# State-space attention and expert layer on one core: B and C of batch 0 by TensorE, halves of delta and du, an earlier last W1 piece, one exponential in PSUM

## The reference, cut to what matters

```python
z = layernorm(x)                                     # gate
u = silu(causal_conv4(in_proj @ ctx) + conv_b)       # 256 channels x 256 steps
dt_lo, Bm, Cm = split(x_proj @ u)                    # 8, 16 and 16 rows x 256 steps
delta = softplus(dt_proj @ dt_lo + dt_proj_b)
state = state * exp(delta[..., None] * A) + (delta * u)[..., None] * B_t     # over the steps, 16 states
y = (state . C_t + D * u) * silu(z);   x = x + y
f = layernorm(x);  probs = softmax(f @ router_w + router_b); top 6 of 32, renormed
x = x + mean of 2 shared experts(f) + sum_e gate_e * expert_e(f)             # relu(f W1 + b1) W2 + b2
```

## Time and profile before

| what | value |
|---|---|
| median of three runs | 386.52 us (384.69 to 386.78) |
| profiled execution | 384.17 us |
| its span | 382.40 us, granted TensorE clock 0.982 in the mean |
| busy: TensorE, VectorE, ScalarE, GpSimd | 358.6, 261.6, 216.7, 201.9 us |
| DMA | 54.20 MB, mean 142 GB/s |

### The profile page before, as it was taken

How to read it: one execution, slowest core, us unless ns; L and a number is a source line. 1 busy time by engine, 2 the same in 40 slices (tenths; PEclk the granted TensorE clock), 3 DMA queues, 4 the chain that set the end, 5 groups by cost and what they waited for, 6 DMA issues and landing times.

```text
span 382.4 us, 6892 instructions
## 1 busy us (share of the span) xinstructions
PE 358.6 (94%) x2301; PEld 320.4 (84%) x2301; DVE 261.6 (68%) x449; ACT 216.7 (57%) x539; POOL 201.9 (53%) x159
## 2 busy tenths in 40 slices
PE   6456889999999999999999999999999999999997
PEld 4233567898999898989999889989999899999996
DVE  3479988899988467499977556899763634344444
ACT  2867755768754445378644456496423346566662
POOL 0479998369993102389961011799830034444442
PEclk9959899999999999999999999999999999999999
DMA  7498871468523215897322235965232144233310
GB/s 233 133 329 240 214 239 44 117 220 283 162 76 87 68 53 136 252 287 206 97 79 82 63 122 155 338 196 141 82 84 82 43 141 139 82 86 89 106 57 27
DMA packets 30751, 54.20 MB, mean 142 GB/s; under 512 B 3298, under 2 KB 8580, under 8 KB 30724
## 3 DMA queue, kind: packets, MB, share of 16 engines
q1 hardware_dynamic: 30724, 53.86, 47.7%
HBM read 52.54 MB, written 1.31 MB: 141 GB/s over the span
## 4 chain that ended last, share of the span: by engine, by line
PE 84%; DMA 5%; DVE 5%; POOL 3%; ACT 2%; issue 1%; SPq 0%; DVEq 0%; POOLq 0%; ACTq 0%
PE acc L549 36%; PE z L570 12%; PE z L571 12%; PE z L572 12%; PE dA L549 4%; DMA bt<-bc 3%; PE acc L447 2%; DVE dA L777 1%; POOL w1l L916 1%; PE acc L556 1%; POOL bu L936 1%; PE misc L469 1%; DMA stage<-in_w 1%; PE dA L483 1%; PE dA L478 1%
## 5 line engine op out<-in xcount | busy, mean ns | idle before, releaser
L549 PE MATMUL acc<-hg,w 128*128 128x256 f32 x564 | 133.5, 379 | 0.0
L702 ACT ACTIVATE z<-z,par 128x256 f32<-128x256 f32 x188 | 75.7, 439 | 86.4 <-PE z L572 86.4
L570 PE MATMUL z<-xh,w1l 128*128 128x256 f32 (+1 forms) x376 | 118.5, 315 | 0.0
L936 POOL TENSOR_TENSOR bu<-bt,du 128x512 f32<-128x512 f32 x64 | 81.0, 1277 | 60.1 <-DMA bt<-bc 43.7
L549 PEld LDWEIGHTS acc<-hg,w 128*128 128x128 f32 x564 | 102.4, 190 | 11.2
L877 DVE TENSOR_TENSOR hg<-z,gt 128x512 f32<-128x512 f32 x88 | 60.5, 688 | 67.7 <-ACT z L702 66.9
L572 PE MATMUL z<-xh,w1h 128*128 128x256 f32 (+1 forms) x376 | 106.2, 282 | 0.0
L571 PE MATMUL z<-xl,w1h 128*128 128x256 f32 (+1 forms) x376 | 105.9, 282 | 0.0
L777 DVE TENSOR_TENSOR_SCAN dA<-dA,bu 128x512 f32<-128x512 f32 x64 | 78.2, 1222 | 9.7 <-POOL bu L936 8.9
L570 PEld LDWEIGHTS z<-xh,w1l 128*128 128x128 f32 x376 | 71.2, 189 | 5.9 <-issue 4.3
L571 PEld LDWEIGHTS z<-xl,w1h 128*128 128x128 f32 x376 | 70.7, 188 | 1.6
(11 more groups left out here) (130 smaller groups left out, 404.1 us busy)
## 6 DMA issues: line engine op xcount, KB each, us to landing
w<-in_w SPq DMA_DIRECT2D x92, 256.0 KB, 2.8
bt<-bc SPq DMA_DIRECT2D x32, 256.0 KB, 5.3
ct<-bc SPq DMA_DIRECT2D x32, 256.0 KB, 6.0
stage<-in_w SPq DMA_DIRECT2D x11, 512.0 KB, 6.8
gt<-gates SPq DMA_DIRECT2D x14, 128.0 KB
xr<-in_xr SPq DMA_DIRECT2D x4, 256.0 KB, 5.8
x<-in_xT SPq DMA_DIRECT2D x4, 256.0 KB, 5.0
out<-x SPq DMA_DIRECT2D x3, 256.0 KB, 7.0
```

Source lines behind the costliest of these rows:

```text
L549: mm = pe.matmul(total(b, k), weights, h, start=t + n == 0 and (k == 0 or final_batch(b)), stop=last, skip_group_check=True)
L570: pe.matmul(z[p % ZB][:, i, :], w1l[:, t, one], xh_, start=k == 0, stop=False)
L702: ins = act.activation(z[p % ZB][:, i, :], z[p % ZB][:, i, :], ACT.Relu, bias=b1[:, t:t + 1])
L936: pool.tensor_tensor(bu[:, r, :].rearrange("p (j l) -> p j l", j=2), bt[:, c % BRING], du[:, k:k + 1, :].broadcast_to([P, 2, L]), ALU.mult ...
```

## The change

- B and C of step 0 of batch 0 no longer come from HBM. A new TensorE step `rows`, behind `dt`, multiplies `xd` by columns of the identity, broadcast over 128 weight columns: each matmul writes one row of `xd` to all partitions, two rows of B to `z[1]`, two of C to `z[2]`. New ScalarE steps `bt0` and `ct0` copy them to `bt[:, 0]` and `ct[:, 0]`. The load `load_bc(0, 0)` goes; the spill stays.
- `delta` and `du` of batch 0 are made by halves. `bu(0,0)` waits for du of half 0 alone, `decay(0,0)` for both halves of delta, and the others for all as before.
- `rs1` moves from before the scans to step 0 (behind `ct0`), `nb1` to step 1, and one `w1h` from before the scans to step 0. Three `warm` steps of nine matmuls are added in steps 5 to 7.
- The last `w1h` and `w1l` move from behind `logits` to behind `econv` of batch 1, ahead of `uclip` and of the root `r2`.
- The exponential of `econv` of batch 1, and the `uclip` behind it, are written to `acc` in PSUM instead of `e1`; `spread`, which writes `acc` next, waits for `usig_done`.

```diff
-        ("dtl", 0), ("w1h", 0), ("w1l", 0), ("dt", 0), ("sp", 0), ("over", 0), ("rs1", 0), ("w1h", 0), ("delta", 0), ("nb1", 0)]
+        ("dtl", 0), ("w1h", 0), ("w1l", 0), ("dt", 0), ("rows", 0), ("sp", 0), ("over", 0), ("bt0", 0), ("delta", 0)]
...
-    HEAD += [(n, 0) for n in ((), (), ("zz",), ("ez1",), ("ez2",), ("ez3",), ("zmul",), ())[_c]]
-    HEAD += [("w1h", 0)] if _c in (1, 2, 4, 5) else []
+    HEAD += [(n, 0) for n in (("ct0", "rs1"), ("nb1",), ("zz",), ("ez1",), ("ez2",), ("ez3",), ("zmul",), ())[_c]]
+    HEAD += [("w1h", 0)] if _c in (0, 1, 2, 4, 5) else []
+    HEAD += [(("warm", None, 9), 0)] if _c > 4 else []
...
-         ("centre", 0), ("sq", 0), ("w1l", 0), (("taps", 3, KC), 1), ("var", 0), ("econv", 1), ("uclip", 1), ("r2", 0),
-         (("warm", None, 31), 0), ("norm", 0), ("usig", 1), ("xh", 0), ("logits", 0), ("w1h", 0), ("w1l", 0), ("u", 1), ("xl", 0),
+         ("centre", 0), ("sq", 0), ("w1l", 0), (("taps", 3, KC), 1), ("var", 0), ("econv", 1), ("w1h", 0), ("w1l", 0),
+         ("uclip", 1), ("r2", 0),
+         (("warm", None, 31), 0), ("norm", 0), ("usig", 1), ("xh", 0), ("logits", 0), ("u", 1), ("xl", 0),
...
-            load_bc(0, 0)
...
+                elif name == "rows":
+                    for row, bank in ((0, z[1]), (NS, z[2])):
+                        for j in range(2):
+                            mm = pe.matmul(bank[:, j, :], ident[0:NBC, row + j:row + j + 1].broadcast_to([NBC, P]), xd[0:NBC, :],
+                                           start=True, stop=True)
+                        mm.then_inc(S["rows_done"], 1)
...
+                    pe.wait_ge(S["usig_done"], 2)
...
-                    act.activation(e1[:], cv[:], ACT.Exp, scale=-1.0).then_inc(S["econv_done"], 1)
+                    act.activation(e_of(b)[:], cv[:], ACT.Exp, scale=-1.0).then_inc(S["econv_done"], 1)
...
-                        act.wait_ge(S["delta_done"], b + 1)
+                        if first(b) and k == 0:
+                            act.wait_ge(S["delta1_done"], 1)
+                        else:
+                            act.wait_ge(S["delta_done"], b + 1)
...
+                elif name == "bt0":
+                    act.wait_ge(S["rows_done"], 1)
+                    act.activation(bt[:, 0], z[1][:], ACT.Copy).then_inc(ld_b[0], 16)
+                elif name == "ct0":
+                    act.wait_ge(S["rows_done"], 2)
+                    act.activation(ct[:, 0], z[2][:], ACT.Copy).then_inc(ld_c[0], 16)
...
-                    dve.tensor_scalar(e1[:], e1[:], BIG, 1.0, ALU.min, ALU.add).then_inc(S["uclip_done"], 1)
+                    dve.tensor_scalar(e_of(b)[:], e_of(b)[:], BIG, 1.0, ALU.min, ALU.add).then_inc(S["uclip_done"], 1)
...
+                        fr.then(dve.tensor_tensor(delta[:, 0, :], xdt[:, 0, :], sp[:, 0, :], ALU.add))
+                        dve.tensor_tensor(du[:, 0, :], delta[:, 0, :], u[:, 0, :], ALU.mult).then_inc(S["du0_done"], 1)
+                        dve.tensor_tensor(delta[:, 1, :], xdt[:, 1, :], sp[:, 1, :], ALU.add).then_inc(S["delta1_done"], 1)
+                        dve.wait_ge(S["delta1_done"], 1)
+                        dve.tensor_tensor(du[:, 1, :], delta[:, 1, :], u[:, 1, :], ALU.mult).then_inc(S["delta_done"], 1)
...
-                        pool.wait_ge(S["delta_done"], b + 1)
+                        pool.wait_ge(S["du0_done" if first(b) and k == 0 else "delta_done"], 1 if first(b) and k == 0 else b + 1)
```

More of the change, by code:

```diff
@@ L216, in xattn_ffn_kernel @@
         aexp_done, aneg_done, const_done = sem("aexp_done"), sem("aneg_done"), sem("const_done")
-        names = ["xin_done", "conv_done", "econv_done", "u_done", "xall_done", "dtl_done", "bc_spilled", "dt_done", "abs_done", "wide_done", "half_done", "half_added", "spread_done",
+        names = ["xin_done", "conv_done", "econv_done", "u_done", "xall_done", "dtl_done", "bc_spilled", "dt_done", "abs_done", "rows_done", "delta1_done", "du0_done", "wide_done", "half_done", "half_added", "spread_done",
                  "v_done", "sp_done", "delta_done", "zz_done", "ez_done", "zmul_done", "bu_done", "da_ready",
@@ L308, in xin, with e_of @@
             return z[ZB - 1] if type(b) is int and b == 1 else misc
+        def e_of(b):
+            return acc if type(b) is int and b == 1 else e1
         def newton(b):
@@ L621, in step @@
                     act.wait_ge(S["uclip_done"], b + 1)
-                    fr.then(act.activation(e1[:], e1[:], ACT.Ln))
+                    fr.then(act.activation(e1[:], e_of(b)[:], ACT.Ln))
                     act.activation(e1[:], e1[:], ACT.Exp, scale=-1.0).then_inc(S["usig_done"], 1)
@@ L769, in step @@
                     fr.wait()
-                    fr.then(dve.tensor_tensor(delta[:], xdt[:], sp[:], ALU.add))
-                    dve.tensor_tensor(du[:], delta[:], u[:], ALU.mult).then_inc(S["delta_done"], 1)
+                    if first(b):
+                        fr.then(dve.tensor_tensor(delta[:, 0, :], xdt[:, 0, :], sp[:, 0, :], ALU.add))
[3 more added lines that the diff above has]
+                        dve.tensor_tensor(du[:, 1, :], delta[:, 1, :], u[:, 1, :], ALU.mult).then_inc(S["delta_done"], 1)
+                    else:
+                        fr.then(dve.tensor_tensor(delta[:], xdt[:], sp[:], ALU.add))
+                        dve.tensor_tensor(du[:], delta[:], u[:], ALU.mult).then_inc(S["delta_done"], 1)
                 elif name[0] == "scan":
```

## The result

Eight runs of the changed kernel took 383.29 to 384.88 us, with a median of 383.91; eight of the kernel before 384.08 to 387.10, with a median of 386.43. The ratio is 0.9947 (95% interval 0.9925 to 0.9968): 2.0 us faster by the ratio, 2.5 by the medians, where I had forecast 0.4. The median lies 0.5 us under the range.

The account below looks back on a forecast made before the run. TensorE was taken as busy throughout from 70 us, so only an earlier first-layer start counts. +0.1 us up to that start and -0.5 behind it give -0.4, 386.52 to 386.1 us; range 384.4 to 387.4.

Parts of the forecast that it names:

- part 3: Layer norm before the first layer: square gains 0.3 to 0.35 us, root waits for the last `w1h`, net +0.1 us.
- The front: First scans without the load of B: first product 0.7 us earlier, but scan(1,0) at 25.5, a loss of 0.25 us.
- The lock: VectorE instructions with two SBUF inputs wait for GpSimd's: `du1` ends at 20.35 instead of 19.5, `nb1` costs 0.8 us.
- GpSimd's end: All twelve w1l pieces done at 64.2 us; before, the eleventh ended at 63.84 and the twelfth at 67.55.
- The square: Square of the layer norm, held to 59.0 us before by a `w1h`; would start at 58.65, gaining 0.3 to 0.35.
- The root: `r2` on ScalarE, behind `econv` and the last `w1h`: starts at 60.85 us, against 60.76 before; the move's price is 0.45.
- The start of the first layer: First L570 matmul on TensorE, at 66.31 us before, forecast at 66.4.
- the cover: Before the Newton steps: `uclip`, 1.52 us before and 0.7 to 0.9 in PSUM, hidden until `r2` is ready at 61.71.
- The signs that I had set: Trace times to confirm the forecast, such as first scan 20.4, square 58.65, `nm` 0.17, or to show a rival instead.
- rival D: The whole gain of the first scans arrives: scan chain 0.9 us earlier, square no longer held; -1.8, 384.7 us; chance 0.11.
- B: Before the first layer: the moved twelfth piece delays `u` and `xl`; +0.7, 387.2 us; chance 0.15.
- C: The last stage transfer is late and ScalarE holds the root until 62.7; 388.0 us; chance 0.05.

Follow-up runs that it names:

- e1: The kernel before, run again with no edit; median 385.48 us, ratio 0.9983; its profile caught a long execution of 386.26 us.
- e2: The kernel before with only the three warm steps of nine matmuls added in scan steps 5 to 7; median 386.33 us, ratio 1.0012.
- e5: The kernel before with only the exponential of `econv` and `uclip` of batch 1 in PSUM; median 383.80 us, ratio 0.9959.
- e9: The kernel before with only step 0's rows and halves and the moved `rs1`, `nb1` and `w1h`; median 384.46 us, ratio 0.9967.
- e6: The kernel before with only the last `w1h` and `w1l` moved ahead of the root, `uclip` still in SBUF; median 388.39 us, ratio 1.0054.
- e4: The kernel before with the last `w1h` and `w1l` moved and batch 1's exponential and `uclip` in PSUM; median 383.67 us, ratio 0.9948.
- e12: The kernel before with the last `w1h`/`w1l` moved, exponential and `uclip` in PSUM, and `u` reading its sigmoid from PSUM; median 383.16 us, ratio 0.9937.
- e10: The changed kernel with `rs1` behind `bt0` and `nb1` behind `delta`; median 382.94 us, ratio 0.9932 to the kernel before.

## Why the prediction was wrong

Against the execution that it was worked from, the sum held: -0.4 us worked out, -0.28 measured. In part that is luck. The two traces are one execution each, and the square in the trace of before was held to 58.96 by a late `w1h`, which the long execution of e1 did not have: there `w1h` started at 56.95 instead of 57.99 and the square at 57.98. The 0.3 us that part 3 takes from this hold is no gain on such executions.

- The front: first scan 20.4 forecast, 20.32 measured; first product 22.0, 21.94; third scan 25.5, 25.36. The lock taken from the one long `hl` priced `du1` and `nb1` rightly.
- GpSimd's end: 64.2 forecast, 63.83 measured; its pieces took 2.33 us each, not the 2.36 counted, which held `uclip`'s share.
- The square: 58.65 forecast, 58.96 measured, from 0.43 us lost at unit 7's product: it starts 0.56 us behind its scan (36.99), where in the kernel before it follows at once (36.43). The trace shows nothing that it waits for. The root: 60.85, 61.00. The start of the first layer: 66.4, 66.53.
- `nm` 0.17 as forecast; `dt` 0.5 us forecast as won, 0.53 measured (0.22 late at the start, 0.31 early at `dt`).

Two steps failed, and both are about `uclip`.

The first is in part 3: "`uclip` in PSUM costs 0.7 to 0.9 [...] and does not wait for GpSimd (1.52 before); both ends are covered, since the Newton steps began at 61.71, when r2 was ready". That was so in this trace by 0.07 us. I took the 1.52 us for the wait's size, when it was the shortest outcome of a race: `uclip` was let in at the first boundary. In e1 and e2 it was not, took 3.45 and 3.57 us, and held the Newton steps for 2.1 and 2.2 us; e5, the kernel before with this edit alone, is 2.1 us faster in the median. I had even written what the cover hid ("once the chain moves earlier this cover would have gone"), and did not ask whether it was there in every run.

The second is in the sum: "The median shown is 386.52, 2.35 above that execution, so 386.1". I carried those 2.35 us over as a constant. They came from this wait, with the clock that fell behind it, and the change removes them. The three runs shown, 386.78, 386.52 and 384.69, with a profile at 384.17, already fell into two groups 2 us apart, which a constant does not explain. The edit whose cost varies from run to run had to be looked for. `uclip` was one such; e9 shows that the front, which moves GpSimd's row and `uclip` against each other, was another.

The signs that I had set could not catch either step, since all of them were read in one execution of the changed kernel: they came out nearly as for a right forecast, while the time was nearest to rival D's.

The Trainium skill had part of the mechanism (VectorE: DVE Perf Modes, "Why PSUM operands drop a tier"): VectorE's double rate for f32 needs both of its SBUF read ports, and an operand in PSUM rules it out. The rows agree with the price: 0.42 us in SBUF where nothing stops it, 0.70 in PSUM in all seven traces that have it there. That `uclip` takes the port shared with GpSimd in SBUF, and not in PSUM, is inferred from that page and the lock cited in the prediction; the rows fit it, 3.45 us in SBUF in e1 and 0.70 beside GpSimd's running row in e5. By both, `uclip` is the instruction at risk. That it can lose its turn to several of GpSimd's instructions one after the other is what the traces of e1, e2 and e6 add.

Of the rivals, B (`u` caught by the moved piece) was seen in e4 (`u`, 0.84 us) and in e12 (`xl`, 0.27), and not in the changed kernel, where GpSimd ended at 63.83 and `u` started at 64.40. C did not occur. Nor did D: the measured 383.91 lies nearest to its 384.7, but the first layer started at 66.53 and not before 65.2, so the time is no sign for it.

## What to carry to other kernels

Where a profiled execution lies 2 us under the median and the runs fall into groups, first find the wait whose length differs between executions: profile the unchanged kernel again until a long execution is caught. A short VectorE instruction that has to wait for GpSimd's instructions, as `uclip` and `nb1` do here, should not be placed beside an unbroken row of long ones; a tile in PSUM (0.28 us more for `uclip`), or a place where GpSimd waits (0.15 us for `nb1` in e10), costs little or nothing. And two edits that shorten the same wait are not worth their sum.

## What the runs showed of the hardware

- A VectorE instruction can miss its turn at a boundary between two GpSimd instructions. `uclip` waited for one of them (1.52 us) and for two (3.45) in executions of the same program, and for three (5.62) in e6.
- An instruction on two numbers a partition waits for GpSimd's running instruction as one on 512 does: `nb1` took 0.15 us or 0.95, `nm` 0.17 or 1.44.
- When VectorE is let in, GpSimd's row is longer by its share: five pieces took 11.62 us without, 11.82 with `uclip` between.
